# A hybrid transformer block on one core: side parts moved around the changes of the output banks, the split of the keys moved into the next head group, norm statistics formed for each half of x

## The reference

```python
x = x + attn_a(ln(x))   # 16 heads of 16, causal softmax, q k v o projections
x = x + ffn(ln(x))      # r = sigmoid(xr W_r); k = relu(xk W_k)^2; r * (k W_v); xr, xk mix each token with the one before
x = x + attn_b(ln(x))   # keys: decaying sum over time, normed per head; values: mix with the next token, normed per head;
                        # queries = keys shifted by one token; causal softmax; output projection
x = x + ffn(ln(x))      # the same weights
```

## Time and profile before

| | |
|---|---|
| median of 3 runs | 3285.78 us (3281.07 to 3286.33) |
| profiled execution | 3280.78 us, span 3279.1 us |
| TensorE busy | 2930.8 us, 89% |
| ScalarE busy | 2236.7 us, 68% |
| VectorE busy | 1459.7 us, 45% |
| GpSimd busy | 866.4 us, 26% |
| TensorE's granted clock, mean | 0.958 of full |

### The profile page before, as it was taken

One profiled execution on the slowest core, in us unless ns is written; L12 is line 12 of the kernel. 1 busy time (PEld: TensorE's weight loads), 2 busy tenths in 40 slices (PEclk: granted clock), 3 DMA queues, 4 the chain that ended last, 5 costly groups with the idle time before them and its releaser, 6 DMA issues.

```text
span 3279.1 us, 99622 instructions
## 1 busy us (share of the span) xinstructions
PE 2930.8 (89%) x42980; PEld 1340.3 (41%) x42980; DVE 1459.7 (45%) x3534; ACT 2236.7 (68%) x2487; POOL 866.4 (26%) x1278
## 2 busy tenths in 40 slices
PE   7799998988998799997999999999888888899887
PEld 3333344434444344443444444444444334433343
DVE  5233235455445643434344333544555555422444
ACT  2588877677777467774777777767676755677562
POOL 4122223332323232221222222232333322322111
PEclk9899999999999799997999999999999998999898
DMA  5222212221222113222222222221222211222111
GB/s 139 83 80 72 88 46 74 63 73 55 77 63 56 54 55 94 73 69 63 88 74 68 76 84 83 68 67 57 59 69 65 77 51 43 68 61 80 44 45 49
DMA packets 229841, 225.66 MB, mean 69 GB/s; under 512 B 33221, under 2 KB 212933, under 8 KB 229320
## 3 DMA queue, kind: packets, MB, share of 16 engines
q1 hardware_dynamic: 228504, 217.47, 23.0%
q10 hardware_dynamic: 816, 0.79, 0.1%
HBM read 146.80 MB, written 71.32 MB: 67 GB/s over the span
## 4 chain that ended last, share of the span: by engine, by line
PE 70%; DVE 11%; issue 8%; POOL 5%; ACT 4%; SPq 1%; DMA 1%; DVEq 0%; ACTq 0%; POOLq 0%
PE ps L860 44%; PE ps L1067 23%; ACT probs L816 4%; POOL probs L719 3%; DVE pmax L1369 2%; PE ps L872 2%; DVE ln_st L1141 1%; DVE xn L1150 1%; POOL buf_a L668 1%; DVE nw_u L1131 1%; DVE nw_u L1133 1%; DVE nw_y L1135 1%; DVE x_buf L1262 1%; DVE xf L1156 1%; DVE o_blk L1411 1%
## 5 line engine op out<-in xcount | busy, mean ns | idle before, releaser
L816 ACT ACTIVATE probs<-ps 128x1024 f32<-128x1024 f32 x2176 | 2087.1, 1072 | 662.6 <-PE ps L860 655.3
L1067 PE MATMUL ps<-probs,v_st 128*17 128x512 f32 (+3 forms) x10240 | 1188.4, 534 | 133.6 <-ACT probs L816 39.9
L860 PE MATMUL ps<-q_st,k_st 99*32 99x512 bf16 (+3 forms) x20480 | 1272.7, 350 | 38.7 <-issue 21.6
L860 PEld LDWEIGHTS ps<-q_st,k_st 99*32 99x32 bf16 x20480 | 587.6, 96 | 819.3 <-issue 465.1
L719 POOL TENSOR_SCALAR_AFFINE_SELECT probs<-probs 128x256 f32<-128x256 f32 (+1 forms) x896 | 440.6, 510 | 1599.7 <-ACT probs L816 1579.2
L1067 PEld LDWEIGHTS ps<-probs,v_st 128*17 128x17 f32 x10240 | 288.9, 98 | 415.4 <-ACT probs L816 100.3
L860 PE MATMUL ps<-xT,wT 128*32 128x512 f32 x2048 | 251.6, 608 | 1.8 <-issue 1.8
L1411 DVE STREAM_TRANSPOSE o_blk<-ps 128x512 f32<-128x512 f32 x128 | 90.8, 709 | 326.5 <-PE ps L1067 326.3
L1286 DVE SCALAR_TENSOR_TENSOR buf_v<-buf_v,ps 128x512 f32<-128x512 f32 x64 | 44.0, 687 | 367.6 <-PE ps L860 367.6
L860 PE MATMUL ps<-wT,o_in 128*32 128x256 f32 x2048 | 144.8, 425 | 47.9 <-issue 47.9
L1262 DVE TENSOR_TENSOR x_buf<-x_buf,ps 128x512 f32<-128x512 f32 x64 | 43.7, 683 | 321.0 <-PE ps L860 321.0
(11 more groups left out here) (136 smaller groups left out, 2180.3 us busy)
## 6 DMA issues: line engine op xcount, KB each, us to landing
part_a<-parts SPq DMA_DIRECT2D x192, 128.0 KB
x_buf<-in_L_attn_a_X SPq DMA_DIRECT2D x32, 512.0 KB, 4.3
q_st<-part_a SPq DMA_DIRECT2D x128, 128.0 KB
o_chan<-o_out SPq DMA_DIRECT2D x64, 256.0 KB, 2.4
o_in<-o_chan SPq DMA_DIRECT2D x64, 256.0 KB, 4.4
q_st<-part_b SPq DMA_DIRECT2D x128, 128.0 KB
k_st<-part_a SPq DMA_DIRECT2D x64, 192.0 KB, 2.9
part_b<-parts SPq DMA_DIRECT2D x96, 128.0 KB
```

The lines of the kernel that those rows point to most:

```text
L816: nc.scalar.activation(probs[:, g % NP_BUF, :], ps[:, bk:bk + 2, :].rearrange("p a n -> p (a n)"), ACT.Exp, scale=SCALE[ATT[g // (NHG * NG ...
L860: last = pe.matmul(o[c:c + 32], kt[:, c:c + 32], q, **how)
L1067: last = pe.matmul(ps[32 * j:32 * j + VW, bank, q0:q0 + w], v_st[:, k % 2, kb, hg * HG + j, :], p, start=(kb == 0), stop=(kb >= TB * qc), ...
```

## The change

Parts are moved to other slots. For M: `t0`, `t1` from slots 9, 11 to 8, 10; `diff` 11 to 10; `shift` 13 to 12; `k0`, `k1` from 16, 18 to 14, 16; `r0` to `f1` from 20 to 26 to 22 to 28; `bt0`, `bt1` from 36, 38 to 34, 36; `bk0` to `bv1` from 40 to 46 to 43 to 49; `vt0`, `vt1` from 51, 53 to 54, 56; `len` 56 to 58; `vb` 62 to 66. The `split` goes from slot 58 to slot 19 of the next head group, `low` from 64, 66 to 22, 24 of the next, `store` from 68, 70 to 26, 28 of the next. For P of batches 2 and 3: `t0`, `t1` from 36, 38 to 35, 37; `u0` to `u3` from 40 to 46 to 43 to 49. The P jobs of batch 1 start in slot 2 of head groups 0 to 3, where they started 19 slots ahead of each. `layernorm` is cut into `statistics` (L1141, for some of the four token blocks) and `normalize`. In an M job the statistics of each half of x follow the addition that completes that half.

```diff
-T_P = {"load": -10, "ln": 0, "t0": 7, "t1": 9, "u0": 11, "u1": 13, "u2": 15, "u3": 17, "v0": 19, "v1": 21, "n0": 24,
-       "n1": 26, "flag": 29, "store": 4, "end": 32}
-T_M = {"load": -10, "o0": 0, "o1": 2, "t0": 13, "t1": 15, "diff": 15, "shift": 17, "k0": 20, "k1": 22, "r0": 24,
-       "r1": 26, "f0": 28, "f1": 30, "out": 33}
-T_B = {"bt0": 40, "bt1": 42, "bk0": 44, "bk1": 46, "bv0": 48, "bv1": 50, "w": 51, "u": 53, "vt0": 55, "vt1": 57,
-       "len": 60, "split": 62, "vb": 66, "low": 68, "store": 72}
+T_P = {"load": -10, "ln": 0, "t0": 6, "t1": 8, "u0": 14, "u1": 16, "u2": 18, "u3": 20, "v0": 22, "v1": 24, "n0": 27,
+       "n1": 29, "flag": 32, "store": 4, "end": 35}
+T_M = {"load": -10, "o0": 0, "o1": 2, "t0": 12, "t1": 14, "diff": 14, "shift": 16, "k0": 18, "k1": 20, "r0": 26,
+       "r1": 28, "f0": 30, "f1": 32, "out": 34}
+T_B = {"bt0": 38, "bt1": 40, "bk0": 47, "bk1": 49, "bv0": 51, "bv1": 53, "w": 54, "u": 56, "vt0": 58, "vt1": 60,
+       "len": 62, "split": 91, "vb": 70, "low": 94, "store": 98}
...
     for c in range(NCH):
-        jobs.append(Job("P", 1, c, 1, start(0, c) + FRONT - T_P["u2"]))
+        jobs.append(Job("P", 1, c, 1, start(0, c) + 2))
...
-                  for name, off in {"P": (("ln", 0),), "MA": (("ln", 2), ("lnb", 30)), "MB": (("ln", 2),)}[j.kind])
+                  for name, off in {"P": (("ln", 0),), "MA": (("ln", 2), ("lnb", 32)), "MB": (("ln", 2),)}[j.kind])
...
-            def layernorm(j):
+            def statistics(j, first, end):
                 x = x_buf[:, j.at["job"] % 2]
-                for tb in range(TB):
+                for tb in range(first, end):
                     step(nc.vector.bn_stats(ln_st[:, tb, :], x[:, tb, :]))
+
+            def normalize(j):
+                x = x_buf[:, j.at["job"] % 2]
                 settle()
...
                     nc.vector.tensor_tensor(half(x, i), half(x, i), ps[:, part.bank, :], ALU.add).then_inc(s_side[part.bank], 1)
-                for i in range(2):
-                    dve.wait_ge(*emptied(j.at[f"o{i}"]))
-                layernorm(j)
+                    dve.wait_ge(*emptied(part))
+                    statistics(j, 2 * i, 2 * i + 2)
+                normalize(j)
...
                                                    ALU.add).then_inc(s_x2, 1)
+                    if j.kind == "MA":
+                        dve.wait_ge(s_x2, 2 * f + i + 1)
+                        statistics(j, 2 * i, 2 * i + 2)
                 if j.kind == "MB":
                     return
-                dve.wait_ge(s_x2, 2 * (f + 1))
-                layernorm(j)
+                normalize(j)
```

More of the change, by code:

```diff
@@ L1204, in p_job @@
                 x_there(j)
-                layernorm(j)
+                statistics(j, 0, TB)
+                normalize(j)
                 if j.b > 0:
```

## The result

The changed kernel takes 3197.96 us, median of 4 runs (3193.39 to 3199.71), against 3286.06 (3281.07 to 3289.05, 4 runs): ratio 0.9731, 95% interval 0.9714 to 0.9748. It is faster by 88 us, where 123 were forecast. 3198 lies in the stated range (3120 to 3218), 37 us above the number given and outside the forecast's own range of 3140 to 3180.

A forecast was written before the change was run, and what follows sets the result against it. TensorE, busy 2930.8 of 3279.1 us, was taken to set the pace, its waits paid nearly in full. Terms -66 -18 -33 -30 +22 +8 +2 -8 gave -123, so 3161 us; range 3120 to 3218, forecast's own 3140 to 3180.

The forecast's parts named there:

- the late second norm: bt0 follows f1 sooner and waits for the norm: 1.4 us 16 times (+22), P jobs 1.0 us 8 times (+8).
- The border: At 14 head-group borders, moving the split removes o1's wait and clock fall: 4.7 us each, 66 us saved.
- the 2 us put down for its new place: Split in slot 19 of the next head group: hidden work, but possibly late stores and reloads, 2 us cost together with `T_END`.
- o1's new wait: At the border, o1 still waits 0.8 us after the change, too short to bring the clock down.
- the lock: VectorE operations with two SBUF inputs and GpSimd SBUF reads exclude each other; apart, the keys' multiply takes 1.1 us, not 2.93.
- The rival of 3213: GpSimd's scaling still runs beside the keys' multiply; o1 waits 2.6 us and the clock falls: 52 us lost, chance 0.13.
- t0 to k1: Earlier diff and k0 remove waits for masks and k1's copy in slots 14 to 19: 1.4 us times 24, 33 saved.
- Slot 40: Emptying bt1 or P's t1 ahead of the take removes the product's wait: 24 times 1.25, 30 us saved.
- the rival of 3192: ScalarE takes up waits removed in slots 14 to 19 and 40; half of 63 us is not won, chance 0.16.
- Halves: Statistics formed by halves end norms 0.7 us sooner; slot 6 gains 0.65 us 24 times, last jobs 3: 18 us saved.
- The rival of 3207: Late norm also brings the clock down: 1.4 us wait and 1.9 of slower matmuls, 24 times, +46 us, chance 0.10.
- The start: Scores start near 91 us, but t0 stands until 115 for batch 1's late x: 8 us saved by head group 4.

The follow-up runs named there:

- split_only: Kernel before the change with only the split of the keys, its low parts and its stores moved into the next head group: 3220.24 us, ratio 0.9797.
- scale_early: Changed kernel with only GpSimd's scaling of the values (vb) put back in slot 62: 3249.9 us, ratio 0.9867.
- ffn_ahead: Kernel before the change with only t0, t1, diff, shift, k0 and k1 of the M jobs moved ahead: 3253.62 us, ratio 0.9905.
- turn_ahead: Kernel before the change with only bt0, bt1 of the MA jobs moved from slots 36, 38 to 34, 36: 3265.5 us, ratio 0.9933.
- whole_stats: Changed kernel with the M jobs' norm statistics formed whole again behind the second half of x: 3229.61 us, ratio 0.9804.
- ffn_end_back: Changed kernel with the M jobs' r0 to f1 back in slots 20 to 26 and the second norm two slots earlier: 3135.4 us, ratio 0.9527.
- p_table: Changed kernel with the slot table of before for the P jobs of batches 0 and 1 alone: 3191.03 us, ratio 0.9702.
- start_moved: Kernel before the change with only the four P jobs of batch 1 moved to slot 2 of head groups 0 to 3: 3275.42 us, ratio 0.9969.
- load_early: Changed kernel with only the first load of x of batch 1 issued where it was before the change: 3180.46 us, ratio 0.9668.

## Why the prediction was right, and by how much off

The direction came out, and the waits went and came where the prediction had them. The sum missed by 35 us, and the time is outside the range that the forecast gave itself. One term, the late second norm, is short by 33 us (63 measured, 30 forecast). That this equals the whole miss is partly luck: others are off both ways, and one cost was not in the sum.

- **The border, -66 forecast.** Right. From the exponential of group 67 to that of group 3 of the next head group, 22 borders into unflagged head groups took 249.4 us and take 182.0; 66.5 us of this are at the 14 with a split. The split alone gave 66, the 2 us put down for its new place don't show, and o1's new wait was forecast at 0.8 us and is 0.69 to 0.97 at four borders. One reason was less than it seemed: the end of GpSimd's overlap wins nothing by itself (`split_only` does without), and what it saves where vt1 stands three slots later no run prices alone. With the scaling early 45 to 52 us are lost, mostly by late masks and the clock (`scale_early`). The multiply takes 1.23 us with GpSimd's scaling apart and 2.92 with it alongside, as the lock has it. The rival of 3213 is out, since the two no longer overlap.
- **t0 to k1, -33.** `ffn_ahead`: -33, but the number agrees partly by luck. Slot 14's wait for its mask stays at 0.79 us, which I had at 0.3, so the waits saved are 0.9 us a head group and not 1.4: 22 us (masks 38.0 to 22.2, "issue" ahead of products 19.6 to 13.3). The rest lies in TensorE's busy time (2930.8 to 2919.6), and its cause stays open.
- **Slot 40, -30.** `turn_ahead`: -21 for 16 of the 24 head groups, with some 4 us of new wait at bt0 in it, which belong to the term of the late norm. For the eight P jobs no run shows the term alone; in the changed kernel no such wait is left at slot 40 of head groups 4 to 27. Both show that ScalarE doesn't take the removed waits up, so the rival of 3192 is out as a cause, though the measured time lies near it.
- **Halves, -18.** Mis-sized both ways. At slot 6 they save 0.4 us and not 0.65 (1.72 to 1.33 us in most head groups), 9 us in all. But `whole_stats` loses 24 to 31 us: most of what the halves are worth is at the late second norm, which I had already counted there.
- **The second norm, late: +22 and +8.** This step failed in size: undoing it is worth 63 us. The waits are 1.95 us in 14 MA head groups and 1.0 in the other two, 29.3 us together (forecast 1.4 each), and 1.79 us at seven of the 8 P jobs (forecast 1.0, though my own rate of 0.87 a slot gives 7.3 - 6.0 = 1.3) and 0.3 at the eighth: 42 us in all. The norm is slower beside the masks. The other large part is the clock, which I had ruled out because waits of 1.7 us had left it alone: it falls behind 6 of the waits of 1.95 us and 2 of those of 1.79 (0.83 over 10 us at 1326 to 1336 and 1916 to 1926). With 1.7 us of full-speed time missing in such a window (0.17 of 10) that is an estimated 14 of the 18.2 us of busy time that `ffn_end_back` saves; the rest isn't assigned. The profile of the kernel before held a sign of it that I overlooked. Of its twelve waits of 1.61 us in slot 40 one brought the clock down, and the product behind it took 1.91 us and not 1.05 as in the earlier trace rows:

```profile
2170.44 1.91 PE L1067 MATMUL ps<-probs,v_st 128*17 128x512 f32 x8 [1.61 <-ACT probs L816]
```

  The rival of 3207 is this cause. It put the fall of the clock at all 24 places, and it is there at 8; the measured time is nearer to it than to 3161. Without this term my sum is -153 us, and `ffn_end_back`, which is the change without it, measured 151 less than the kernel before of the first comparison (155 by its ratio). Here too, errors of other terms cancel.
- **The start, -8.** The stretch up to head group 4 gains 2 us (first exponential there at 415.77, before 418.08; my terms add up to 413 and not 411, as four P jobs at 15 are 60). x late by the order of SP's queue was right: t0 was forecast to stand until 115, and did until 116.69. What I left out is that the new P table also holds for batch 0, ahead of slot 0, where there are no bank changes to avoid: flags are done at 93.40, 5.6 us later than in the earlier trace rows. `p_table` gives 6 us of it back ahead of the first exponential, and 1.6 behind it.
- **Not foreseen: four borders into flagged head groups, +12.** The waits ahead of the first row-maxima matmul L987 go from 40.6 to 52.8 us:

```profile
1068.24 0.26 PE L987 MATMUL ps<-k_st,q_st 99*128 99x128 bf16 x1 [12.56 <-issue]
```

They are 40.6 to 41.3 us in `split_only`, `ffn_ahead` and `turn_ahead`, and 49.8 to 52.8 in all kernels in which the P jobs of batch 1 have moved, `start_moved` (49.8) among them. The largest increases are ahead of the last two (9.2 to 12.9 us, 9.4 to 15.5). By the trace's records of TensorE's sequencer most of these waits is compare-and-branch: the one into the block (L1098), the four on single heads (L1003) and some ahead of them take 32.7 us in the kernel before and 43.9 in the changed one. It isn't one branch that got slow. In the kernel before the four of L1003 take 0.2, 1.7 to 2.2, 0.2 and 0.07 us (much the same in the three others in which the P jobs stay), in the kernels with moved P jobs 2.6 to 3.3, 0.2, 1.3 to 2.0 and 0.07. That moving P jobs does it is shown. Why is open: that instructions lie elsewhere and have to be fetched anew is only argued.

One account stays open too. The single gains on the kernel before (66, 33, 21, 11) and the costs undone on the changed one don't add up to 88 exactly: 66 + 33 + 21 + 11 + 9 (halves at slot 6) - 63 - 7 (table) = 70. That the P jobs' share of slot 40 is missing in the 21, and that the parts share waits, would both explain a part; the 18 us aren't assigned.

## What to carry to other kernels

When parts are moved apart, look at what was squeezed between them: without the late norm the change wins 151 us, 66 of them by taking long VectorE work out of a tight chain, and it gave 63 back by making another chain (f1, norm, bt0) shorter than it needs: 5.2 us for TensorE where the norm takes 7.1. Before calling a wait too short to matter for the clock, look at all waits of its length in the profile at hand, and not at one. Where an engine runs in order, ask at each wait for it what short duty stands behind a long one: one line that lets a take go ahead of a norm won 26 us. And a table of offsets tuned for one surrounding (bank changes) should not be applied where that surrounding is missing.

## What the runs showed of the hardware

- Waits of TensorE of the same length bring the granted clock down in some places and not in others. Behind the 14 waits of 1.95 us at bt0 it fell 6 times in the changed kernel, 11 in `scale_early`, 3 in `load_early` and 6 in `p_table`; behind the 14 waits of 2.67 us in `whole_stats` 11 times; behind the 12 waits of 1.61 us of slot 40 in the kernel before once. In the changed kernel TensorE is busy for the same 8.27 us of 10 where it fell and where it didn't. The Trainium skill (TensorE: Matmul & The Clock Gate, "Part 1: The HAM clock gate (the "warmup" mystery)") says that the hardware's look at TensorE's activity isn't started anew with a kernel, so that the point at which the clock changes varies from run to run; that the same waits fare differently from place to place and from run to run fits this. A price for a wait should hold a share of clock loss, not all or nothing.
- The last four operations of a norm on VectorE (128x256) take 1.73 us with four masks of GpSimd alongside and 1.38 without.
- A compare-and-branch of TensorE took 0.22 us or 1.3 to 2.0 us in the same place (the third of L1003) as the P jobs stood in other slots, another one 1.7 to 2.3 us or 0.22, and the one into the flagged block 4.4 to 5.4 us in every kernel. The Trainium skill (Advanced Engine Details and Errata, "Control Flow Timing") gives about 108 ns for a compare-and-branch, which none of these agrees with.
